# Gate layer in four column groups and window values by pairs of patches, in a fused attention and expert kernel

## The reference

```python
# window branch: the image padded to 35 x 35, in 25 patches of 7 x 7 = 49 tokens
qkv = (xw @ qkv_w + qkv_b).reshape(bw, ws * ws, 3, HEADS, HD)   # v = xw @ Wv: 49 x 128 a patch
# gate: three factors for each pixel
g = sigmoid(gelu(xs @ gate_w1 + gate_b1) @ gate_w2 + gate_b2)   # 1024x128 @ 128x32, then @ 32x3
out = g[..., 0:1] * out_cmp + g[..., 1:2] * out_slc + g[..., 2:3] * out_win
```

## Time and profile before

| | |
|---|---|
| median of three runs | 842.24 us (840.95 to 847.28) |
| profiled execution | 840.26 us, its span 838.5 us |
| mean granted clock of TensorE | 0.907 of full |
| opening | to 64 us |
| images 0 to 3, up to the end of the seam | 64, 203, 344 and 489 us to 640 us |
| experts and output | 640 us to the end |

### The profile page before, as it was taken

How to read it: one execution, slowest core, us unless ns; L and a number is a source line. 1 busy time by engine, 2 the same in 40 slices (tenths; PEclk the granted TensorE clock), 3 DMA queues, 4 the chain that set the end, 5 groups by cost and what they waited for, 6 DMA issues and landing times.

```text
span 838.5 us, 17744 instructions
## 1 busy us (share of the span) xinstructions
PE 666.8 (80%) x5228; PEld 500.0 (60%) x5229; DVE 514.0 (61%) x1719; ACT 418.8 (50%) x1238; POOL 239.5 (29%) x406
## 2 busy tenths in 40 slices
PE   2998899986889989688998966787631599999953
PEld 1684476654557556355755643553430599998952
DVE  4208378938857884875887568679763244444434
ACT  1327634663742554554356455326311388887842
POOL 3100043001013730201472010345015356565630
PEclk9999999997999999689999979957965799999985
DMA  9100000001000000000010170011022122222236
GB/s 315 58 1 26 1 6 1 2 1 51 2 1 5 27 27 6 21 0 2 5 33 20 34 195 0 4 37 42 2 76 64 48 64 63 69 63 63 63 128 219
DMA packets 34288, 38.63 MB, mean 46 GB/s; under 512 B 11668, under 2 KB 27044, under 8 KB 33956
## 3 DMA queue, kind: packets, MB, share of 16 engines
q1 hardware_dynamic: 28660, 26.77, 10.7%
q0 software_dynamic: 4416, 9.00, 3.0%
q10 hardware_dynamic: 1152, 2.10, 0.7%
HBM read 24.94 MB, written 13.98 MB: 46 GB/s over the span
## 4 chain that ended last, share of the span: by engine, by line
PE 52%; DVE 24%; issue 6%; ACT 6%; POOL 5%; DMA 4%; SPq 2%; DVEq 0%; POOLq 0%; ACTq 0%
PE ps L1919 7%; PE ps L1903 7%; PE ps L1483 6%; PE ps L1488 6%; PE ps L1537 5%; PE ps L1594 4%; DVE nmx L1060 4%; PE ps L1621 3%; DVE t_tok L1186 3%; DVE x_tok L1045 3%; PE ps L1552 3%; DVE r_P L1070 3%; PE ps L1524 2%; POOL xs_d L651 2%; DMA qTs<-z_d 2%
## 5 line engine op out<-in xcount | busy, mean ns | idle before, releaser
L783 ACT ACTIVATE r_P<-ps,nmx 128x225 f32<-128x225 f32 (+1 forms) x192 | 85.9, 467 | 58.2 <-DVE nmx L1060 58.2
L946 ACT ACTIVATE R<-ps,R 128x128 f32<-128x128 f32 x292 | 83.5, 368 | 44.9 <-PE ps L1903 44.9
L687 POOL DMA_INDIRECT z_d<-R x72 | 69.4, 964 | 67.1 <-DVE R L1445 49.8
L1483 PE MATMUL ps<-ident,r_P 128*128 128x128 f32 (+1 forms) x384 | 59.0, 291 | 32.7 <-ACT R L796 14.6
L574 POOL TENSOR_TENSOR rstd<-vpe,minus_half 128x8 f32<-128x8 f32 x8 | 13.3, 1658 | 236.7 <-DVE vpe L1006 236.7
L1483 PEld LDWEIGHTS ps<-ident,r_P 128*128 128x128 f32 (+1 forms) x384 | 47.0, 155 | 56.1 <-issue 29.1
L1919 PE MATMUL ps<-w_sb,R 128*128 x576 | 79.3, 280 | 0.0
L1060 DVE TENSOR_REDUCE nmx<-ps 128x4 f32<-128x900 f32 (+1 forms) x64 | 73.2, 1153 | 9.8 <-PE ps L1594 9.6
L1903 PE MATMUL ps<-R 128*128 128x128 f32 x584 | 78.9, 279 | 0.0
L1903 PEld LDWEIGHTS ps<-R 128*128 128x128 f32 x584 | 72.4, 195 | 0.0
L651 POOL DMA_INDIRECT xs_d<-pay,pos x64 | 63.0, 985 | 32.6 <-issue 18.9
(11 more groups left out here) (225 smaller groups left out, 1335.7 us busy)
## 6 DMA issues: line engine op xcount, KB each, us to landing
R<-xs_d SPq DMA_DIRECT2D x76, 65.0 KB, 1.8
x_sb<-x SPq DMA_DIRECT2D x4, 512.0 KB, 3.5
w_sb<-w1k SPq DMA_DIRECT2D x1, 2048.0 KB, 8.8
w_sb<-w1v SPq DMA_DIRECT2D x1, 2048.0 KB, 13.2
w_sb<-fw SPq DMA_DIRECT2D x1, 2048.0 KB, 9.9
w_sb<-fw SPq DMA_DIRECT2D x4, 512.0 KB, 10.5
out<-x_tok ACTq DMA_DIRECT2D x8, 256.0 KB, 2.3
t_d<-t_tok SPq DMA_DIRECT2D x3, 512.0 KB, 2.6
```

The costliest lines, as they stand in the source:

```text
L687: gp.indirect_dma_start(z_d, bass.IndirectOffsetOnAxis(wd[:, r, 1:2].bitcast(U32), 0), yrow[:, r, :], None).then_inc(y_out[r], 16)
L783: last = sc.activation(Pb[t % NRING][:, h, 0:m], bank(name)[:, (h % 2) * m:(h % 2) * m + m], ACT.Exp, bias=nmx[:, t % NRING, h:h + 1], acc ...
L946: last = sc.activation(hT[:, r % 2, c, :], hid(r)[:, C * c:C * c + C], ACT.Gelu, bias=wx[:, r, O_B1 + c:O_B1 + c + 1])
L1483: last = tr(bank(name)[0:m, k * j:k * j + k], src, ident[0:k, 0:k])
```

## The change

The gate's first weights stay 32 wide. Four products of 256 pixels each write their own 32 PSUM partitions of one bank; one gelu of 128 x 256 follows, with the bias repeated four times. The second weights lie four times on the diagonal of a 128 x 12 matrix, so two products of 128 weight columns give all eight pixel tiles. VectorE adds the bias in two instructions. The values take two patches a product: `xwin` has 64 columns a patch, 15 of them zero, so 128 weight columns cover a pair, and a bank takes four pairs. The second patch of a pair lands in partitions 64 to 112, and ScalarE copies a bank in two instructions, one for each half. There are four groups of eight patches (the last has one patch), at t = 2, 3, 9 and 10.

```diff
@@
-    own = {2: ("qw0", "vw0"), 3: ("vw1",), 4: ("vw2", "qw1"), 8: ("vw3", "qw2"), 9: ("vw4", "vw5"), 10: ("vw6",)}
+    own = {2: ("qw0", "vw0"), 3: ("vw1",), 4: ("qw1",), 8: ("qw2",), 9: ("vw2",), 10: ("vw3",)}
@@
-        gw1_sb = sb("gw1_sb", [128, 128])
-        gw2_sb = sb("gw2_sb", [128, 3])
+        gw1_sb = sb("gw1_sb", [128, GH])
+        gw2_sb = sb("gw2_sb", [128, NQ * 3])
@@
-        xwin = sb("xwin", [128, NWIN, WTOK])
+        xwin = sb("xwin", [128, NWIN, WPAD])
@@
-            pool.wait_ge(zeroed, 5)
-            pool.dma_start(gw1_sb[:, 0:GH], gate_w1).then_inc(win_in, 16)
-            pool.dma_start(gw2_sb[0:GH, :], gate_w2).then_inc(win_in, 16)
+            pool.wait_ge(zeroed, 4)
+            pool.dma_start(gw1_sb[:, :], gate_w1).then_inc(win_in, 16)
+            for q in range(NQ):
+                pool.dma_start(gw2_sb[GH * q:GH * q + GH, 3 * q:3 * q + 3], gate_w2).then_inc(win_in, 16)
@@ scalar
             def window_values(b, g):
-                n = min(4, NWIN - 4 * g)
-                copy_out(f"vw{g}@{b}", vw[:, 4 * g:4 * g + n, :].rearrange("p w c -> p (w c)"),
-                         bank(f"vw{g}@{b}")[0:WTOK, 0:n * C])
+                name = f"vw{g}@{b}"
+                act.wait_ge(*filled(name))
+                for j in range(2):
+                    n = len(range(8 * g + j, min(8 * g + 8, NWIN), 2))
+                    if n:
+                        last = sc.activation(vw[:, 8 * g + j:min(8 * g + 8, NWIN):2, :],
+                                             bank(name)[WPAD * j:WPAD * j + WTOK, 0:n * C].rearrange("p (w c) -> p w c", c=C), ACT.Copy)
+                last.then_inc(read_sem(name), 1)
@@
-            def gate_hidden(h, i):
-                name = f"gh{i}@{h}"
+            def gate_hidden(h):
+                name = f"gh@{h}"
                 act.wait_ge(*filled(name))
-                sc.activation(gh[:, 512 * i:512 * i + 512], bank(name), ACT.Gelu, bias=col("gate_b1")).then_inc(read_sem(name), 1)
+                sc.activation(gh[:, 0:QTOK], bank(name)[:, 0:QTOK], ACT.Gelu, bias=col("gate_b1")).then_inc(read_sem(name), 1)
@@ vector
-                ve.tensor_tensor(ge[:, :, :], bank(name)[:, 2 * C:2 * C + 3 * NT].rearrange("p (t g) -> p t g", g=3),
-                                 rows[:, ROW_GB:ROW_GB + 3].unsqueeze(1).to_broadcast([128, NT, 3]), ALU.add)
+                for j in range(NT // NQ):
+                    at_ = 2 * C + 3 * NQ * j
+                    ve.tensor_tensor(ge[:, j:NT:NT // NQ, :], bank(name)[:, at_:at_ + 3 * NQ].rearrange("p (q g) -> p q g", g=3),
+                                     rows[:, ROW_GB:ROW_GB + 3].unsqueeze(1).to_broadcast([128, NQ, 3]), ALU.add)
@@ tensor
             def gate_hidden(h):
-                for i in range(2):
-                    project(f"gh{i}@{h}", gw1_sb[:, :], pixels(i), 512)
+                name = f"gh@{h}"
+                claim(name)
+                for q in range(NQ):
+                    last = mm(bank(name)[GH * q:GH * q + GH, 0:QTOK], gw1_sb[:, :], xhatT[:, QTOK // W * q:QTOK // W * (q + 1), :],
+                              start=True, stop=True)
+                last.then_inc(full_sem(name), 1)
@@
-                for w in range(4 * g, min(4 * g + 4, NWIN)):
-                    last = mm(bank(name)[0:WTOK, C * (w % 4):C * (w % 4) + C], xwin[:, w, :],
+                for i, w in enumerate(range(8 * g, min(8 * g + 8, NWIN), 2)):
+                    nw = min(2, NWIN - w)
+                    last = mm(bank(name)[0:WPAD * nw, C * i:C * i + C], xwin[:, w:w + nw, :].rearrange("p w m -> p (w m)"),
                               qkvw_sb[:, 2 * C:3 * C], start=True, stop=True)
@@
-                for t in range(NT):
-                    mm(bank(name)[:, 2 * C + 3 * t:2 * C + 3 * t + 3], gh[:, 128 * t:128 * t + 128], gw2_sb[:, :],
+                for j in range(NT // NQ):
+                    at_ = 2 * C + 3 * NQ * j
+                    mm(bank(name)[:, at_:at_ + 3 * NQ], gh[:, 128 * j:128 * j + 128], gw2_sb[:, :],
                        start=True, stop=True)
```

More of the change, by code:

```diff
@@ L40 @@
 GH = C // 4
+NQ = 4
+QTOK = N // NQ
+WPAD = 64
 SIDE = 2 * WS - 1
 NWIN = GRID * GRID
+NVW = (NWIN + 7) // 8
 NPAIR = (NWIN + 1) // 2
@@ L111, in psum_plan @@
     every = around(range(8))
-    every(*(f"{n}@0" for n in ("xt0", "xt1", "xh0", "xh1", "kc0", "kc1", "vc0", "vc1", "qc0", "qc1", "gh0", "gh1",
+    every(*(f"{n}@0" for n in ("xt0", "xt1", "xh0", "xh1", "kc0", "kc1", "vc0", "vc1", "qc0", "qc1", "gh",
                                "kw0", "kw1", "kw2")), "pb", "mk@0", "pc", "mv@0", "k2@0", "gv@0", "qs0@0", "qs1@0")
@@ L155, in psum_plan @@
             if t == NT and h < B:
-                put(0, f"gh0@{h}")
-                put(1, f"gh1@{h}")
+                put(0, f"gh@{h}")
             if t == NT + 1 and h < B:
@@ L461, in _ @@
             sp.dma_start(qkvw_sb[:, :], wqkv_w).then_inc(proj_in, 16)
-            sp.wait_ge(zeroed, 5)
+            sp.wait_ge(zeroed, 4)
             for j in range(2):
@@ L601, in windows_of_image @@
                         last = gp.tensor_copy(
-                            xwin[:, GRID * wr + wc:GRID * wr + wc + nw, :].rearrange("p w (r c) -> p w r c", r=WS)[:, :, 0:nr, 0:ncol],
+                            xwin[:, GRID * wr + wc:GRID * wr + wc + nw, 0:WTOK].rearrange("p w (r c) -> p w r c", r=WS)[:, :, 0:nr, 0:ncol],
                             xhatT[:, WS * wr:WS * wr + nr, WS * wc:WS * wc + nw * ncol].rearrange("p r (w c) -> p w r c", w=nw))
@@ L749, in key_blocks @@
                 act.wait_ge(*filled(name))
-                act.wait_ge(zeroed, 6)
+                act.wait_ge(zeroed, 5)
                 for k, (mask, bias) in enumerate((("even", "b2ke"), ("odd", "b2ko"))):
@@ L819, in opening @@
                     queries(f"qc{i}@0", qT, i, 0)
-                for i in range(2):
-                    gate_hidden(0, i)
+                gate_hidden(0)
                 window_keys(0, 1)
@@ L864, in compressed_tiles @@
                     if t == 8:
-                        window_values(b, 3)
                         window_queries(b, 2)
                     if t == 9:
-                        window_values(b, 4)
-                        window_values(b, 5)
+                        window_values(b, 2)
                     if t == 10:
-                        window_values(b, 6)
+                        window_values(b, 3)
             def window_stage(b):
@@ L903, in selected_tiles @@
                         hidden_from_bank(f"mv@{h}", hv, [col(f"b1v{a}") for a in range(2)])
-                        for i in range(2):
-                            gate_hidden(h, i)
+                        gate_hidden(h)
                     if t == NT + 1 and h < B:
@@ L1512, in gate_hidden @@
             def gate_hidden(h):
-                for i in range(2):
-                    project(f"gh{i}@{h}", gw1_sb[:, :], pixels(i), 512)
+                name = f"gh@{h}"
[4 more added lines that the diff above has]
+                last.then_inc(full_sem(name), 1)
             def window_projection(b, name, k, i):
                 w0, nw = WPARTS[i]
-                project(f"{name}{i}@{b}", qkvw_sb[:, C * k:C * k + C], xwin[:, w0:w0 + nw, :], nw * WTOK)
+                project(f"{name}{i}@{b}", qkvw_sb[:, C * k:C * k + C], xwin[:, w0:w0 + nw, 0:WTOK], nw * WTOK)
             def window_values(b, g):
@@ L1572, in compressed_values_and_gates @@
                 name = f"gv@{h}"
-                for i in range(2):
-                    pe.wait_ge(*copied(f"gh{i}@{h}"))
+                pe.wait_ge(*copied(f"gh@{h}"))
                 claim(name)
                 pe.nop(nofuse=True)
-                for t in range(NT):
-                    mm(bank(name)[:, 2 * C + 3 * t:2 * C + 3 * t + 3], gh[:, 128 * t:128 * t + 128], gw2_sb[:, :],
+                for j in range(NT // NQ):
+                    at_ = 2 * C + 3 * NQ * j
+                    mm(bank(name)[:, at_:at_ + 3 * NQ], gh[:, 128 * j:128 * j + 128], gw2_sb[:, :],
                        start=True, stop=True)
@@ L1708, in opening @@
                 block_projection(0, "qc", 0)
-                pe.wait_ge(win_in, 32)
+                pe.wait_ge(win_in, 16 * (1 + NQ))
                 gate_hidden(0)
@@ L1970 @@
         cols[at, COL["b2k" + name[0]]] = p["cmpk_b2"][at]
-    put("gate_b1", p["gate_b1"])
+    put("gate_b1", np.tile(p["gate_b1"], NQ))
     half = (np.arange(128) // NPOS) % 2
```

11 lines of the change are left out of this document (2 added, 9 removed).

## The result

| | before | after |
|---|---|---|
| median of the runs | 844.47 us (840.95 to 847.28, 4 runs) | 831.98 us (831.33 to 833.31, 4 runs) |
| profiled execution, its span | 840.26, 838.5 us | 833.31, 831.3 us |
| mean granted clock of TensorE | 0.907 | 0.896 |

The ratio is 0.988 with a 95% interval of 0.984 to 0.991: 12.5 us by the medians. The profiled execution of before is shorter than its four timed ones and that of after is the longest of its four, so the profiles show only 7.2 us of span. That is what can be placed.

The account below looks back on a forecast made before the run. TensorE's chain in the opening and a PE-ScalarE handshake in the tiles were taken as the bound. Gains 2.42 + 4.35 + 5.76 + 1.41 = 13.9 us gave 826.3 or 828.3; forecast 827.5, range 823 to 835, chance 0.72.

Parts of the forecast that it names:

- rival B: Compressed tiles: extra copies plus VectorE eat the values' gain, only the gate's 6.8 us stay, time 834.7; chance 0.13.
- rival C: Compressed tiles: TensorE's clock stays low, each group costs 0.87 us more; from 16 groups the 13.9 is gone; chance 0.03.
- Gate groups: Opening: four 32-column products of 256 take 0.55 us instead of 1.71; gain 1.16.
- rival A: Gate: column groups don't overlap in so short a burst, four take 1.71 us; total gain 9.3, about 832; chance 0.08.
- Second layer: Opening: the gate's eight tiny products become two, taking 0.42 us; gain 1.26.
- Opening in all: Opening: both gate savings count in full on PE's unbroken chain, 2.42 us.
- Gate at the end of the selected tiles: Images 0 to 2: shorter gate and one gelu bring the transposes 1.45 us sooner each; 4.35 us.
- Values, price of a group: Compressed tiles: a group of eight patches costs 0.99 us, what one of four did; bounds 0.84 and 1.67.
- Rival D: Weight loads are on the path; three groups an image take back 0.6 us each, 2.5 in all, 830; chance 0.04.
- Values, the extra copy: Compressed tiles, steps 2 and 3: ScalarE's second copy of a group adds 0.49 us each to the handshake.
- Values, steps 4, 8 and 9: Compressed tiles: groups gone at steps 4 and 8, shorter at 9; gains 1.00, 1.01 and 0.89 us.
- Values, images 2 and 3: Compressed tiles: 1.92 us less in image 2, 1.41 less in image 3, where step 4's gain is lost.

Follow-up runs that it names:

- the gate alone: Only the gate's half of the change put into the kernel before, values as before: 831.18 us, ratio 0.987.
- the values alone: The kernel before with only the window values of the changed kernel: 844.66 us, ratio 1.002.
- the two profiles: Two profiled executions of the whole change, the second from running it again unedited; that repeat measured 831.9 us, ratio 0.991 to the kernel before.
- the kernel with one copy: The changed kernel with only the first of ScalarE's two copies of a bank, odd patches using the even neighbour's values: 823.24 us, ratio 0.978.
- Useless products: The changed kernel with image 3's scores of tile 6 made twice and of tile 7 four times: 829.58 us, ratio 0.986.
- ScalarE's new order: ScalarE copies the turned probabilities before the extras: changed kernel 808.09 us, ratio 0.959; kernel before 826.67 us, ratio 0.980.

## Why the prediction was right, and where its terms were off

The time came within the range, 4.5 us above the forecast. The direction and the gate's mechanism held; the values' terms for images 2 and 3 and the extra copy were mis-sized.

That the total fell so near is in part luck. Of the 13.9 us, 6.8 were the gate's and 7.2 the values'. By the medians the gate alone gains 9.7 us, more than its terms, and the values alone nothing (1.002 [0.998, 1.006]): the two errors partly cancel in the sum. The time lies nearer to rival B's 834.7 than to the forecast, and what made it so is the mechanism of rival C.

In spans the forecast was 13.9 us and the profiles show 7.2. The 6.7 us between them are: opening 1.45, images 0 and 1 0.3, image 2 1.6, image 3 2.7, gate 0.35, the end 1.2, less 0.9 that the window stage gave unasked.

- **Gate groups.** Right: 0.57 against 0.55, and rival A is out. Left out of the sum was what the groups cost their neighbours, 0.09 ahead and 0.11 behind: the gain is 0.95 against 1.16. That switching the tiling mode drains TensorE is a rule of the Trainium skill, TensorEngine Tiling (Array Packing), Key Properties. The trace agrees in so far as each change between full width and groups is dearer than a step within either, by these 0.09 and 0.11 us.
- **Second layer.** 0.35 against 0.42.
- **Opening in all.** 0.97 in the first profile and 1.84 in the second, against 2.42. The gate's terms gave 0.95 + 1.33 = 2.28; what took a part back was the clock of the projections ahead of it, whose twelve records take 5.72 to 7.30 us in the eleven traces of this study in which they have a row of their own. In all eleven that length, less half of the time from their start to the first clock record, is 5.23 or 5.24 us. So the whole difference is the stretch at the 1.2 GHz level, and it accounts for the two profiles: 2.28, plus 0.15 and 0.05 for an earlier start, less 1.46 and 0.49 for the longer low stretch, is 0.97 and 1.84. The Trainium skill, TensorE: Matmul & The Clock Gate, What's actually happening, says that the number of slow matmuls at a kernel's start changes from run to run; the traces agree, with a first clock record between 19.69 and 23.59 us. The sum had no term for it.
- **Gate at the end of the selected tiles.** 1.33 to 1.34 against 1.45, within its bounds, and the seam behind kept it. Of the difference 0.09 is the step into the groups again: the gate's first record starts before the transposes ahead of it end, by 0.16 before and by 0.07 now.
- **Values, price of a group.** 0.90 to 1.01 against 0.99. Rival D, weight loads on the path, is out.
- **Values, the extra copy.** Mis-sized: taken as 0.49, 0.59 less an overlap of 0.10. The two copies lie 0.60 apart, and the way from group to transposes is 0.63 longer in step 2 and 0.73 in step 3, or 0.75 by the kernel with one copy. The 0.10 of overlap was read from a gelu and the copy behind it, not from two copies.
- **Values, steps 4, 8 and 9.** They give what was forecast, a little more in fact (1.77 in all, though the two copies cost 0.63 and 0.73 instead of 0.49 each, so these steps give 3.13 against 2.90). Rival B's first half, the copies, was a part of the truth; VectorE was not in the way. In step 8 of image 1 its rows do stand on the chain now, from 236.34 to 237.25, in place of ScalarE's, and the step is shorter all the same.
- **Values, images 2 and 3.** This is the term that failed. Forecast were 1.92 and 1.41 less, measured 0.32 less and 1.31 more. Rival C had named the mechanism, the clock, and given it 0.03, since the clock was high before and the work removed was 3 us of about 30. It came at a part of its size: image 3's 2.7 us and image 2's 1.6, 4.3 in all, about five of the sixteen groups of 0.87 from which it was to decide. Against it I had set the clock slices; they showed only where the low level fell with the work of before. Image 2 of before, at 0.84 with its group at 1.89, was the sign that the kernel stood at the edge.
- **The gate's share by the medians.** The gate alone gains 9.7 us, while its terms add up to 6.3 (0.95 + 1.33 + 3 x 1.34). The rest I can't place, since the one profile of that kernel is not of a typical execution. Nor is it settled what decides in which image the low level falls.

The window stage of image 1 gave 0.62 us unasked. The chain of before has SyncE's issues and a load of block rows there, up to 267.18, and that of after has not.

## What to carry to other kernels

Before saving matmuls in front of a PSUM handshake, count the evacuations that the new layout needs: the products saved 1.0 us a step here and each second copy took 0.6 to 0.75 back. Have the engine that frees the awaited bank do that first and copy everything else behind it; on this kernel that was worth more than the whole change (23.8 us against 12.5), and made the change worth more as well. Where a trace has no clock record yet, read TensorE's level from the distance of equal records and not from the clock column. And where the granted clock of a stretch is already below full, forecast less TensorE work there with its own case for the clock, and compare two kernels only on stretches with the same granted clock.

## What was not expected of the hardware

- Less TensorE work can cost time: with the values alone the granted clock of images 1 to 3 was 0.80, 0.80 and 0.73 where before had 0.92, 0.84 and 0.87, and the ratio was 1.002. Useless products bring it back: 0.78 to 0.92 in image 3, 45.54 to 40.75 us. With ScalarE's new order, fewer products did not lower the mean clock.
- In the opening the views print a clock of 1.00 where the trace has no clock record yet. TensorE's records ran at half rate there, up to the first clock record, at 19.69 to 23.59 us; between two traces this alone moved the opening by up to 1.6 us.
- Four 32-column groups between full-width products took 0.57 us, and 0.09 and 0.11 more in their neighbours.
- Two ScalarE copies of 49x512 from one bank start 0.60 us apart, and the copy of 97x512 behind them starts 0.02 us after the second ends, where behind a single one it starts about 0.1 before the end.
- One chip took 3% longer for the kernel before (867.84 against 840.88, 843.45 and 842.37 us elsewhere). The kernels profiled there wait beside GpSimd's scatters, 5.80 us at a time in the row shown.
